# Cross attention of a wide block: probability transposes as two 64-row tiles, and the order of TensorE's work inside a step

## The reference, cut to what matters

```python
q = layer_norm(x, g2, be2) @ wq2          # 128 x 1280, 20 heads of 64
k, v = context @ wk2, context @ wv2       # 77 x 1280
scores = einsum('bhnd,bhmd->bhnm', q, k) * 64 ** -0.5
attn = softmax(scores, axis=-1)           # 128 x 77 for a head and a sequence
out = einsum('bhnm,bhmd->bhnd', attn, v)
x = out.reshape(b, n, 1280) @ wo2 + bo2 + x
```

## Time and profile before

| | |
|---|---|
| median of three runs | 3640.47 us |
| the profiled execution, its own time | 3640.09 us |
| its span, first to last instruction | 3638.3 us |
| TensorE busy | 3565.8 us (98%) |
| stage c1, first scores to last output projection | about 2346.5 to 3383.7 us |

### The profile page before, as it was taken

The page is one execution under the profiler, slowest core; times in us unless marked ns, Lnnn a source line. Parts: engine busy times, 40 slices in busy tenths (PEclk is TensorE's granted clock), DMA queues, the critical chain, the costliest instruction groups (busy, mean ns, idle before and its releaser), DMA issues. The chain is left out here.

```text
span 3638.3 us, 93033 instructions
## 1 busy us (share of the span) xinstructions
PE 3565.8 (98%) x37535; PEld 3078.2 (85%) x37535; DVE 2316.8 (64%) x3902; ACT 2073.9 (57%) x5150; POOL 1255.6 (35%) x1278
## 2 busy tenths in 40 slices
PE   8999999999998999999999999799999999999999
PEld 6777787878887898989889898688888888888888
DVE  5788866664554666666667676566666666666554
ACT  5777777774335555555555555455555555555333
POOL 5333333331443333333333333322233222333432
PEclk9999999999999999999999999999999999999999
DMA  4444332322001000000000000100000000000000
GB/s 108 104 121 101 94 91 77 93 75 73 0 0 35 2 1 2 2 2 1 2 2 1 2 2 1 25 4 3 4 3 3 4 3 4 3 3 2 20 22 22
DMA packets 99740, 101.44 MB, mean 28 GB/s; under 512 B 31248, under 2 KB 74128, under 8 KB 99344
## 3 DMA queue, kind: packets, MB, share of 16 engines
q1 hardware_dynamic: 93408, 94.41, 10.2%
q0 software_dynamic: 5120, 1.35, 0.2%
q10 hardware_dynamic: 816, 0.08, 0.0%
HBM read 20.76 MB, written 5.24 MB: 7 GB/s over the span
## 5 line engine op out<-in xcount | busy, mean ns | idle before, releaser
L1250 POOL TENSOR_TENSOR a_probs<-a_probs,a_rsums 128x1024 f32<-128x1024 f32 x160 | 303.9, 1899 | 752.1 <-DVE a_rsums L1407 752.1
L1288 ACT ACTIVATE a_probs<-a_scores_banks,a_negmax 128x128 f32<-128x128 f32 x1280 | 367.4, 377 | 284.0 <-DVE a_negmax L1395 284.0
L1288 ACT ACTIVATE c_probs<-c_scores_banks,c_negmax 128x77 f32<-128x77 f32 x1280 | 317.6, 350 | 251.4 <-DVE c_negmax L1395 251.1
L1250 POOL TENSOR_TENSOR c_probs<-c_probs,c_rsums 128x616 f32<-128x616 f32 x160 | 197.8, 1236 | 729.9 <-DVE c_rsums L1407 729.9
L724 ACT ACTIVATE s_probs<-s_scoresT_banks 128x1024 f32<-128x1024 f32 (+1 forms) x320 | 327.6, 1024 | 181.4 <-PE s_scoresT_banks L901 179.2
L810 DVE TENSOR_REDUCE s_negmax<-s_scores_banks 128x8 f32<-128x1024 f32 (+1 forms) x320 | 322.4, 1007 | 135.5 <-PE s_scores_banks L883 131.3
L1388 DVE COPY a_outT<-a_out_bank 128x512 f32<-128x512 f32 x160 | 110.7, 692 | 294.2 <-PE a_out_bank L1605 239.4
L1789 DVE SCALAR_TENSOR_TENSOR f_hidden<-f_value_bank,bias,f_gate 128x512 f32<-128x512 f32 x160 | 120.1, 750 | 247.2 <-ACT f_gate L1764 245.2
L679 POOL DMA_DIRECT2D s_q_stack<-s_shift x160 | 93.8, 586 | 488.0 <-ACT s_shift L747 481.6
L1395 DVE TENSOR_REDUCE a_negmax<-a_scores_banks 128x4 f32<-128x512 f32 x320 | 206.2, 686 | 86.9 <-PE a_scores_banks L1475 86.9
L1764 ACT ACTIVATE f_gate<-f_gate_bank,bias 128x512 f32<-128x512 f32 x160 | 110.1, 688 | 260.6 <-PE f_value_bank L325 260.5
(11 more groups left out here) (306 smaller groups left out, 10405.0 us busy)
## 6 DMA issues: line engine op xcount, KB each, us to landing
s_q_stack<-front SPq DMA_DIRECT2D x192, 160.0 KB, 3.3
s_k_stack<-front SPq DMA_DIRECT2D x96, 160.0 KB, 3.8
s_out<-s_heads SPq DMA_DIRECT2D x128, 80.0 KB, 2.6
s_k_stack<-front SPq DMA_DIRECT2D x96, 96.2 KB, 2.9
x_tokens<-in_x SPq DMA_DIRECT2D x16, 320.0 KB, 3.6
out_x<-x_tokens SPq DMA_DIRECT2D x16, 320.0 KB, 2.4
s_q_stack<-s_shift POOLq DMA_DIRECT2D x160, 8.0 KB, 2.6
s_ctx_in<-in_ctx SPq DMA_DIRECT2D x16, 115.5 KB
```

Of the source, the lines that this page charges most:

```text
L1250: nc.gpsimd.tensor_tensor(probs[i][:], probs[i][:], rsums[(k - 1) % 2][:].unsqueeze(2).broadcast_to([P, UNIT, NK]), ALU.mult).then_inc(s_p ...
L1288: done = nc.scalar.activation(probs[i][:, h, :], scores[:, h // GROUP, h % GROUP * NK:(h % GROUP + 1) * NK], ACT.Exp, bias=negmax[k % 2][: ...
```

## The change

In stage c1 alone:

- `transpose_step` makes two transposes for each head instead of one: tokens 0 to 63 from array rows 0 to 63 into bank 0 of `pt`, and tokens 64 to 127 from rows 64 to 127 into bank 1. Sixteen transposes of 64 x 77 with 64 moving columns take the place of eight of 128 x 77 with 128. VectorE's copy to `probsT` reads and writes runs of 64 elements.
- TensorE's order in a step: scores, transposes, head outputs (now of unit k-3, `Y_LAG`, instead of k-2), norm transposes, queries, early key tile, output projection, late key tile, values, context transposes (at the end of step 4 instead of in step 5).
- VectorE: maxima first, then the copy to `outT`, then (step 5) the context's low part.
- ScalarE: the norm's affine part comes after the late key tile instead of first.
- Key tiles: 3 moves from step 8 to 7, 7 from step 2 (early) to 1 (late), 8 becomes early and 9 late in step 2; the waits on `s_k` and `done.s_y` follow.

```diff
-        KEYS_EARLY = {6: 1, 7: 2, 9: 4, 0: 5, 1: 6, 2: 7}
-        KEYS_LATE = {5: 0, 8: 3, 2: 8, 3: 9}
+        KEYS_EARLY = {6: 1, 7: 2, 9: 4, 0: 5, 1: 6, 2: 8}
+        KEYS_LATE = {5: 0, 7: 3, 1: 7, 2: 9}
...
-                if s == 3 and which:
+                if s == 3 and which and not cross:
                     which.scalar_affine(act, ahead, par, odd_bank, (s_vproj, (pair_of(q, k) + 1) * GROUPS))
...
                     keys_out(q, k, KEYS_LATE)
+                    if s == 3 and which:
+                        which.scalar_affine(act, ahead, par, odd_bank, (s_vproj, (pair_of(q, k) + 1) * GROUPS))
...
+                if cross:
+                    outputs_copy(n - Y_LAG)
+                double = both_at(q, k)
+                if k == GROUPS and double is not None:
+                    dve.wait_ge(crossing.s_high, 2 * double + 2)
+                    nc.vector.tensor_tensor(ctx_low[0:CTX_D, :], odd_bank[0:CTX_D, 0:QUAD * NKC],
+                                            ctx_high[0:CTX_D, :].bitcast(F32), ALU.subtract).then_inc(s_ctx_split, 2)
...
+                    if cross:
+                        nc.vector.tensor_copy(probsT[0:NK, :, :].rearrange("p h (half t) -> p half h t", half=2),
+                                              pt[0:NK, :, :].rearrange("p half (h t) -> p half h t", t=dh)).then_inc(s_probsT, 1)
...
-                    last = nc.tensor.transpose(pt[0:NK, h // GROUP, h % GROUP * P:(h % GROUP + 1) * P], probs[k % 5][:, h, :], m.ident[:])
+                    if cross:
+                        for half in range(2):
+                            rows = slice(dh * half, dh * half + dh)
+                            last = nc.tensor.transpose(pt[0:NK, half, h * dh:(h + 1) * dh], probs[k % 5][rows, h, :], m.ident[rows, rows])
...
-                    if k % BODY in (3, 8):
-                        pe.wait_ge(done.s_y, 2 * (BASE + capped(pair_of(q, k) + 3, PAIRS)))
+                    if t == 4:
+                        pe.wait_ge(done.s_y, 2 * (BASE + pair_of(q, k) + 3))
...
                 scores_step(q, k)
+                if cross:
+                    transpose_step(q, k - T_LAG)
+                    values_step(q, k - Y_LAG)
...
-                        pe.wait_ge(s_k, TILES * q + (9 if k == 3 else TILES + 3))
+                        pe.wait_ge(s_k, TILES * q + (TILES if k == 3 else TILES + 4))
...
+                if cross:
+                    project_queries(q, k)
+                    project_keys(q, k, KEYS_EARLY)
+                    output_step(q, k - Y_LAG)
+                    project_keys(q, k, KEYS_LATE)
+                    project_values(q, k)
...
                 double = both_at(q, k)
-                if k == GROUPS and double is not None:
-                    pe.wait_ge(s_k, TILES * double)
+                if k == GROUPS - 1 and double is not None:
+                    pe.wait_ge(done.s_y, 2 * (BASE + pair_of(q, k) + 3))
```

More of the change, by code:

```diff
@@ L1373, in _, with outputs_copy @@
         def _(dve):
+            def outputs_copy(n):
+                if live(n, WUNITS):
+                    dve.wait_ge(s_out, n + 1)
+                    if due(n):
+                        dve.wait_ge(s_y, n)
+                    nc.vector.tensor_copy(outT[:], out_bank[:]).then_inc(s_outT, 1)
             def step(q, k):
@@ L1378, in step @@
                     which.wait_stats(dve, ahead)
-                double = both_at(q, k)
-                if k == GROUPS and double is not None:
[L1381 to L1388, removed]
+                if not cross:
+                    outputs_copy(n - Y_LAG)
                 if live(n, WUNITS):
@@ L1411, in step @@
                         dve.wait_ge(s_out, n - T_LAG)
[L1412 removed]
+                    if cross:
+                        nc.vector.tensor_copy(probsT[0:NK, :, :].rearrange("p h (half t) -> p half h t", half=2),
+                                              pt[0:NK, :, :].rearrange("p half (h t) -> p half h t", t=dh)).then_inc(s_probsT, 1)
+                    else:
+                        nc.vector.tensor_copy(probsT[0:NK, :, :].rearrange("p (j h) k -> p j (h k)", j=2),
+                                              pt[0:NK, :, :]).then_inc(s_probsT, 1)
                 if live(n - Y_LAG, WUNITS) and (k - Y_LAG) % GROUPS == GROUPS - 1:
@@ L1487, in transpose_step @@
                 for h in range(UNIT):
-                    last = nc.tensor.transpose(pt[0:NK, h // GROUP, h % GROUP * P:(h % GROUP + 1) * P], probs[k % 5][:, h, :], m.ident[:])
+                    if cross:
+                        for half in range(2):
+                            rows = slice(dh * half, dh * half + dh)
+                            last = nc.tensor.transpose(pt[0:NK, half, h * dh:(h + 1) * dh], probs[k % 5][rows, h, :], m.ident[rows, rows])
+                    else:
+                        last = nc.tensor.transpose(pt[0:NK, h // GROUP, h % GROUP * P:(h % GROUP + 1) * P], probs[k % 5][:, h, :],
+                                                   m.ident[:])
                 last.then_inc(s_pt, 1)
@@ L1629, in step @@
                     last.then_inc(crossing.s_T, 1)
+                if cross:
[4 more added lines that the diff above has]
+                    project_values(q, k)
+                else:
+                    transpose_step(q, k - T_LAG)
+                    output_step(q, k - Y_LAG)
+                    project(q, k, 0)
+                    project(q, k, 1)
+                    project_values(q, k)
+                    values_step(q, k - T_LAG)
                 double = both_at(q, k)
-                if k == GROUPS and double is not None:
-                    pe.wait_ge(s_k, TILES * double)
+                if k == GROUPS - 1 and double is not None:
+                    pe.wait_ge(done.s_y, 2 * (BASE + pair_of(q, k) + 3))
                     for i in range(2):
```

13 lines of the change are left out of this document (1 added, 12 removed).

## The result

The changed kernel takes 3609.12 us in the median of five executions, the kernel before 3639.7 us in the same rounds. Four of the five lie between 3601.33 and 3616.36 us; the fifth, a disturbed one of 3734.41 us, is left out of the ratio, which is 0.9914 with a 95% interval of 0.9892 to 0.9936. A second measurement, in other rounds, gave 0.9907 (0.9872 to 0.9941). The forecast was 3588 us with a range of 3563 to 3624. Direction and range hold; the gain is 31 to 37 us where 52 were worked out.

The account below looks back on a forecast made before the run. Stage c1 was taken to cost what TensorE's own instruction list costs. From 3640.1 us, 46.4 for the transposes and 6 for waits were taken off, giving 3587.7, stated as 3588 us, range 3563 to 3624.

Parts of the forecast that it names:

- The transposes: Stage c1, TensorE: sixteen row-half transposes at 65 to 73 ns a pair, 0.58 us instead of 0.87; 46.4 us saved.
- The seams: Tiling changes on TensorE: three a step before and after, costed at nothing; 0.1 us a step either way, 16 us in all.
- The waits of step 5: Step 5 of a double: waits removed by the new order, about 0.4 us in each of 15 doubles; 6 us saved.
- a risk to the values' copy: ScalarE: affine part, some 1.7 us, pushes this copy to about 2.1 us into the next step; next bank writer starts at 2.7.
- ScalarE's chain: Query copy to last exponential takes 1.79 us, ending 5.66 into the step; next scores at about 5.97, so 0.3 us cover.
- The first rival: ScalarE's chain binds: run 0.5 us longer, 0.2 us a step comes back, 3620 us; chance 0.17, shared with dearer seams.
- The ends of the stage and the clock: Last five steps of c1: head outputs' wait for probsT gives way to one for outT, taken as 0.
- the 61.3: Sign expected in the changed kernel's profile: ten steady steps of c1 in 61.3 us, TensorE idle under 1 us in them.
- The copy to `probsT`: VectorE's copy in runs of 64: costed as before, 1.2 us; twice as slow it would cost 30 us in all.

Follow-up runs that it names:

- experiment 3: The changed kernel with the head outputs of unit k-2 at the end of the step, as before the change; ratio 0.9920 to the kernel before, ten steps 61.36 us.
- experiment 1: The kernel before with the row-half transposes alone, in their old place between key products and output projection; ratio 1.0000, ten steps 64.96 us.
- experiment 4: The kernel before with only the key tiles' new steps, context transposes ending step 4, and VectorE's low part behind the maxima; ratio 1.0033, ten steps 65.33 us.
- experiment 5: As experiment 4, with the norm's affine part also behind the late key tile in ScalarE's queue; ratio 0.9992 to the kernel before, ten steps 64.35 us.
- experiment 6: The changed kernel with the norm's affine part first in ScalarE's step again; one execution 3656.23 us, ten steps 63.95 us at the full clock.
- experiment 2: The changed kernel with the old eight whole-array transposes between scores and head outputs; ratio 1.0052 to the kernel before, ten steps 65.79 us.
- experiment 8: The changed kernel with key tile 3 back in step -2 for the five steps before unit 0 alone; 3604.72 us.
- experiment 9: The changed kernel run again, unedited; median 3603.21 us, the profiled execution 3657.69 us.
- experiment 7: The changed kernel with three unused products behind the values of each of the five steps before unit 0; median 3592.09 us, ratio 0.9823 to the kernel before.

## Why the prediction was right, and where it fell short

**The transposes: right.** Forecast 65 to 73 ns a pair, 0.58 us for all; measured 69 ns, and 0.64 us to the next start, with the seam to the head outputs in it, while the scores before them gave up theirs (0.95 instead of 1.05). Scores and transposes together: forecast 1.63, measured 1.59. The two of a pair start 7 ns apart, so two row halves do load side by side.

That a pair is bound by one load fits the rows. From a pair with 128 columns loaded and 77 moved (scores, 112 ns) to one with 77 loaded and 64 moved (69 ns) the pace falls by 43 ns for 51 loaded columns, 0.84 ns a column, as the load records' slope had it; for the 13 moved columns it would be 3.3 ns each, where a whole transpose with 128 moved takes 109 ns. The moving part alone would be 55 ns, half of that 109. An estimate from the Trainium skill (TensorE: Matmul & The Clock Gate, LDWEIGHTS) is 77 / 1.2 = 64 ns for such a load; the measured pair takes 5 ns more. No run changes load and moving part separately.

**The seams: right, and they were the point.** Costing three seams for three was correct, and by experiment 3 their direction costs nearly nothing. What I said only in passing, that the transposes left in place would have paid two seams more, turned out to be a whole sum of its own: with them in place the gain is zero (experiment 1).

**The waits of step 5: a term with the wrong reason.** I had 6 us for the contexts' move. Step 5 does give back 0.75 us, but step 4 takes 0.41, and the moved key tiles bring 0.4 us twice without taking it from steps 3 and 8 as long as the affine part stands first (experiment 4). With that part late the term is 0.51 us a double, 8 us (experiment 5). The prediction listed the affine part only as a risk to the values' copy; it was a needed edit, worth 2.8 us a double in the final order (experiment 6).

**ScalarE's chain: cover as laid out.** In the step shown above:

```profile
2822.63 0.59 ACT L1299 COPY c_qk<-c_even_bank 128x512 f32<-128x512 f32 x1 [1.17 <-PE c_even_bank L325]
2823.11 0.42 ACT L1307 COPY c_keys<-c_odd_bank 128x308 f32<-128x308 f32 x1
2823.42 0.99 ACT L1288 ACTIVATE c_probs<-c_scores_banks,c_negmax 128x77 f32<-128x77 f32 x4
```

The exponentials end at 2824.41, and the next scores start at 2824.74: 0.33 us, forecast 0.3. The first rival didn't happen.

**The ends of the stage and the clock: the step that failed.** "In the last five steps, with no projections, the wait of the head outputs for probsT gives way to one for outT; I take 0." Measured 8.65 us, with new waits of 2.12 and 2.41 us for GpSimd, since the transposes now stand ahead of everything that used to cover them, and a lower clock (0.85 against 0.95). The exchange that the sentence names did come out, eight waits of 0.79 us for `outT` in place of six for `probsT`, and it cost 1.6 us; GpSimd's waits cost 3.9. How the rest divides between clock and work isn't shown. For the first steps I wrote nothing; they cost 11.1 us, all of it clock.

Without these 20 us the profiled execution would have been at 3583. The sum was nearly right for the steady part and wrong in that it took it for the whole. For ten steps its own terms give 64.85 - 2.9 - 0.4 = 61.55 us, and 61.12 were measured; the 61.3 named at the prediction's end doesn't follow from them. Over 16 doubles the steady part so gave 7 us more than the sum, which hid a third of the loss at the ends. That the median with fillers at both ends, 3588.1, is the number forecast for the change alone is in part luck: its end is still 5.8 us longer than before the change.

**The copy to `probsT`**: 1179 ns in the median, no dearer in runs of 64 (1220 before). The stages before and after c1 kept their time in the two profiles: unit 0 starts within 0.24 us, and from the end of c1 to the end it is 254.5 us in both.

## What to carry to other kernels

Splitting the transposes over row halves paid here only beside other work in the same tiling. So count the seams in a step before and after (the two here cost 0.18 us together, the one of experiment 2 0.16) and let like stand by like. When a group is moved ahead, the in-order queue behind it changes on the other engines too: four ScalarE instructions left where they were would have cost three quarters of the steady gain. And a gain worked out for the steady loop has to be checked where the pipeline fills and drains, where covers are missing and TensorE may lose its clock; with a few unused products there, and one group of transposes moved, most of the loss came back, and the four executions agreed within 6 us.

## What was not expected of the hardware

The clock, once low, stayed low for some 37 us although TensorE was busy for 9 to 10 of every 10 us. What makes it fall isn't settled: it fell with windows of 7.0 and 7.9 us busy of 10 and held with 6.7 and 7.7, both in the kernel before and in experiment 8. Such stretches, in stages that the change doesn't touch, also lie behind the 54 us of experiment 9 and the 18.7 of experiment 7.

GpSimd's multiplication of the probabilities takes 1.22 us in most steps, and in steps 4 and 9 of the changed kernel 2.42, while VectorE's split of the norm beside it takes 1.43 us instead of 0.48. GpSimd and VectorE in a step 4:

```profile
2811.19 2.42 POOL L1250 TENSOR_TENSOR c_probs<-c_probs,c_rsums 128x616 f32<-128x616 f32 x1 [4.72 <-DVE c_rsums L1416]
```

```profile
2812.13 0.41 DVE L196 TENSOR_TENSOR pair_low<-pair_y,pair_high 128x256 fp32r<-128x256 f32 x1
2812.46 1.43 DVE L198 SCALAR_TENSOR_TENSOR pair_stack<-pair_yhigh,minus_low_row,pair_y 128x256 fp32r<-128x256 f32 x1
```

Before the change the two never overlapped in time. The other profiles bear out that they slow one another: wherever in c1 the split (the second VectorE line) overlaps the multiplication it takes 1.43 us, and elsewhere 0.48. In halves_alone both happen in the same program, with 15 of the 30 splits each; there the multiplication takes 2.59 us when overlapped. No run tells how the two block each other. It has a price: the multiplication ends at 2813.61, and the transposes of step 5 start only at 2813.67, 1.08 us after the scores instead of 0.95:

```profile
2812.59 1.12 PE L1489 MATMUL c_scores_banks<-c_keys,c_qk 64*128 64x77 f32 x16
2813.67 0.77 PE L1505 MATMUL c_pt_banks<-ident,c_probs 64*77 64x64 f32 x16
```
